# DLRM interaction and tower on one core: TensorE raises its semaphores once per several results instead of once per result

## The reference, cut to what matters

```python
# B = 2048 samples, D = 128, F = 26 tables; ids (2048, 26)
e = stack([tbl_f[ids[:, f]] for f in range(26)], axis=1)          # (B, 26, 128)
combined = concatenate([dense[:, None, :], e], axis=1)            # (B, 27, 128)
interactions = einsum('bfd,bgd->bfg', combined, combined)         # all dots of a sample's 27 vectors
z = concatenate([dense, interactions[:, IU0, IU1]], axis=1)       # the 351 pairs above the diagonal
h = concatenate([z, dense], axis=1)                               # (B, 607)
h = maximum(h @ W_top1 + b_top1, 0)                               # (B, 512)
h = maximum(h @ W_top2 + b_top2, 0)                               # (B, 256)
y = h @ W_top3                                                    # (B, 1)
```

## Time and profile before

| | |
|---|---|
| median of 3 runs | 691.15 us (689.26 to 691.96) |
| span of the profiled execution, first to last instruction | 677.5 us |
| PE busy | 423.8 us, 63% |
| POOL (gathers) busy | 275.0 us, 41% |
| DVE busy | 239.6 us, 35% |
| ACT busy | 170.0 us, 25% |
| mean granted TensorE clock | 0.758 |

### The profile page before, as it was taken

One profiled execution on the slowest core, in us unless ns is written; L12 is line 12 of the kernel. 1 busy time (PEld: TensorE's weight loads), 2 busy tenths in 40 slices (PEclk: granted clock), 3 DMA queues, 4 the chain that ended last, 5 costly groups with the idle time before them and its releaser, 6 DMA issues.

```text
span 677.5 us, 8517 instructions
## 1 busy us (share of the span) xinstructions
PE 423.8 (63%) x2992; PEld 403.1 (59%) x2992; DVE 239.6 (35%) x700; ACT 170.0 (25%) x366; POOL 275.0 (41%) x297
## 2 busy tenths in 40 slices
PE   2525354856947279471795726957269571784997
PEld 2415253855946179471794726956269471783997
DVE  5725210762504335043260432603434052530334
ACT  2204120431314024030231401313023040230551
POOL 6771737054172701727017271172712727036000
PEclk9967676786986659766597665976679575896899
DMA  8930211431114311243012430124301152001440
GB/s 222 275 93 14 71 31 50 83 108 43 51 52 83 90 29 44 55 86 87 15 48 53 81 92 12 54 51 81 94 28 48 52 99 74 19 23 50 85 64 23
DMA packets 61247, 46.01 MB, mean 68 GB/s; under 512 B 45677, under 2 KB 51301, under 8 KB 61228
## 3 DMA queue, kind: packets, MB, share of 16 engines
q1 hardware_dynamic: 52012, 26.87, 17.8%
q0 software_dynamic: 9216, 18.89, 10.8%
HBM read 37.20 MB, written 8.53 MB: 67 GB/s over the span
## 4 chain that ended last, share of the span: by engine, by line
PE 49%; another core or an unknown queue 34%; issue 11%; ACT 2%; DMA 2%; DVE 2%; SPq 1%; ACTq 0%; DVEq 0%
PE looked_up L406 20%; PE dot_bank L445 9%; PE mlp_bank L465 7%; PE mlp_bank L498 3%; PE turned L427 3%; PE turned L445 3%; PE looked_up L427 2%; DMA whole_tables<-in_tbl 2%; PE mlp_bank L508 1%; ACT dots L591 1%; PE dot_bank L427 1%; DVE whole_hidden L773 1%; ACT high_tables L635 1%; DVE combined L739 0%
## 5 line engine op out<-in xcount | busy, mean ns | idle before, releaser
L372 POOL DMA_INDIRECT rows<-in_tbl,tile_ids x288 | 273.7, 950 | 347.0 <-DVE tile_ids L736 262.4
L406 PE MATMUL looked_up<-one_hot,high_tables 125*128 125x256 f32 x512 | 144.0, 314 | 46.0 <-issue 23.4
L445 PE MATMUL dot_bank<-combined 128*108 128x108 f32 x768 | 99.4, 287 | 77.9 <-issue 41.8
L406 PE MATMUL looked_up<-one_hot,low_tables 125*128 125x256 f32 x512 | 141.6, 310 | 8.1 <-issue 8.1
L723 DVE TENSOR_SCALAR one_hot<-spread_ids,chunk_row 128x256 fp32r<-128x256 int32 x448 | 126.5, 359 | 52.6 <-remote 42.2
L406 PEld LDWEIGHTS looked_up<-one_hot,high_tables 125*128 125x128 f32 x512 | 113.0, 221 | 49.0 <-issue 49.0
L445 PEld LDWEIGHTS dot_bank<-combined 128*108 128x108 f32 x768 | 90.3, 197 | 84.1 <-issue 46.0
L406 PEld LDWEIGHTS looked_up<-one_hot,low_tables 125*128 125x128 f32 x512 | 112.7, 220 | 8.9 <-issue 8.9
L591 ACT COPY dots<-dot_bank 108x432 f32<-108x432 f32 x96 | 49.3, 519 | 242.3 <-remote 151.7
L773 DVE TENSOR_SCALAR whole_hidden<-mlp_bank,bias 128x256 f32<-128x256 f32 x28 | 13.5, 481 | 161.5 <-remote 99.1
L445 PE MATMUL turned<-combined 128*108 128x108 f32 x256 | 33.8, 281 | 47.2 <-issue 47.2
(11 more groups left out here) (73 smaller groups left out, 451.9 us busy)
## 6 DMA issues: line engine op xcount, KB each, us to landing
spread_ids<-in_ids_by_feature SPq DMA_DIRECT2D x28, 256.0 KB
scratch<-dots SPq DMA_DIRECT2D x28, 208.0 KB
rows<-in_tbl,tile_ids POOLq DMA_INDIRECT x288
whole_tables<-in_tbl SPq DMA_DIRECT2D x8, 448.0 KB
whole_hidden<-scratch SPq DMA_DIRECT2D x24, 117.0 KB
scratch<-dots SPq DMA_DIRECT2D x28, 52.0 KB
rows<-in_r_dense_features SPq DMA_DIRECT2D x16, 64.0 KB
first_ids<-in_ids_by_feature SPq DMA_DIRECT2D x1, 896.0 KB, 8.5
```

The source lines that it names most:

```text
L372: nc.gpsimd.indirect_dma_start(rows[:, u, slot, :], None, tables[f][:, :], bass.IndirectOffsetOnAxis(ap=tile_ids[:, u, slot - 1:slot], axi ...
L406: last = nc.tensor.matmul(looked_up[n % 2][:, 0:COLS], parts[part][0:ROWS_K, n, c, :], one_hot[0:ROWS_K, n % HOT, c, :], start=(c == 0 and ...
L445: last = nc.tensor.matmul(dot_bank[b % DOT_BANKS][0:SQUARE, q * SQUARE:(q + 1) * SQUARE], quad, quad, start=True, stop=True)
```

## The change

TensorE's signals are merged; a merged signal adds as many counts as it stands for, so that the readers' counts stay as they were. Transposes signal after group 1 (two counts) and after group 4 (three). Dots signal after fills 2, 5 and 7 (three, three and two counts). `half_used` is gone; `product_done` is raised after every second look-up by two, two look-ups now share one PSUM bank (256 columns each), and a look-up of an even number from 4 on waits for the copies of all look-ups up to number `n - 3`. Layer 1 signals after outputs 1 and 3 by two, layer 2 once by two, and the last block's layer 1 once by four. Readers are unchanged but for the one-hots, which wait once, for `product_done` of look-up `n-3`.

```diff
+LOOKS_PER_BANK = 2
+TURNED_SIGNALS = {1: 2, N_GROUPS - 1: N_GROUPS - 2}
+DOTS_SIGNALS = {2: 3, 5: 3, 7: 2}
...
-        half_used = sem("half_used")
...
+        def look_view(n):
+            at = n % LOOKS_PER_BANK * COLS
+            return looked_up[n // LOOKS_PER_BANK % 2][:, at:at + COLS]
...
-                    if n >= 2:
-                        pe.wait_ge(product_copied, m * N_PRODUCT + n - 1)
+                    if n >= 2 * LOOKS_PER_BANK and n % LOOKS_PER_BANK == 0:
+                        pe.wait_ge(product_copied, m * N_PRODUCT + n - LOOKS_PER_BANK)
...
-                        if c == CHUNKS // 2 - 1:
-                            last.then_inc(half_used, 1)
-                    last.then_inc(product_done, 1)
+                    if n % LOOKS_PER_BANK == LOOKS_PER_BANK - 1:
+                        last.then_inc(product_done, LOOKS_PER_BANK)
...
-                    last.then_inc(turned_done, 1)
+                    if g in TURNED_SIGNALS:
+                        last.then_inc(turned_done, TURNED_SIGNALS[g])
...
-                    last.then_inc(dots_done, 1)
+                    if b in DOTS_SIGNALS:
+                        last.then_inc(dots_done, DOTS_SIGNALS[b])
...                                                            (layer1)
-                    last.then_inc(layer_done, 1)
+                    if o % 2 == 1:
+                        last.then_inc(layer_done, 2)
...                                                            (last_layer1)
-                    if tiles[-1] == K_TILES - 1:
-                        last.then_inc(layer_done, 1)
+                if tiles[-1] == K_TILES - 1:
+                    last.then_inc(layer_done, LAYER1)
...                                                            (layer2)
-                    last.then_inc(layer_done, 1)
+                last.then_inc(layer_done, LAYER2)
...                                                            (make_one_hots)
                     if n >= HOT and c == 0:
-                        dve.wait_ge(half_used, m * N_PRODUCT + n - HOT + 1)
-                    if n >= HOT and c == CHUNKS // 2:
                         dve.wait_ge(product_done, m * N_PRODUCT + n - HOT + 1)
```

More of the change, by code:

```diff
@@ L400, in look_up_products @@
                         pe.wait_ge(table_split, n + 1)
-                    if n >= 2:
-                        pe.wait_ge(product_copied, m * N_PRODUCT + n - 1)
+                    if n >= 2 * LOOKS_PER_BANK and n % LOOKS_PER_BANK == 0:
+                        pe.wait_ge(product_copied, m * N_PRODUCT + n - LOOKS_PER_BANK)
                     for c in range(CHUNKS):
                         for part in (HIGH, LOW):
-                            last = nc.tensor.matmul(looked_up[n % 2][:, 0:COLS], parts[part][0:ROWS_K, n, c, :],
+                            last = nc.tensor.matmul(look_view(n), parts[part][0:ROWS_K, n, c, :],
                                                     one_hot[0:ROWS_K, n % HOT, c, :],
@@ L563, in copy_products @@
                     act.wait_ge(product_done, m * N_PRODUCT + n + 1)
-                    nc.scalar.copy(combined[:, 0, :, PRODUCT_SLOT + n], looked_up[n % 2][:, 0:P])
-                    nc.scalar.copy(ahead[:, n, :], looked_up[n % 2][:, P:COLS]).then_inc(product_copied, 1)
+                    nc.scalar.copy(combined[:, 0, :, PRODUCT_SLOT + n], look_view(n)[:, 0:P])
+                    nc.scalar.copy(ahead[:, n, :], look_view(n)[:, P:COLS]).then_inc(product_copied, 1)
             def move_ahead(m, products):
```

## The result

The changed kernel takes 729.68 us (median of 4 runs, 723.71 to 733.46) where the kernel before took 690.2 us beside it (median of 4): ratio 1.0581, 95% interval 1.0503 to 1.0660, 39.5 us slower. The forecast was 733 us and 42.1 us slower. The profiled execution is the one of 733.46 us.

The account below looks back on a forecast made before the run. TensorE's matmuls were taken to wait in line beside two gathers a block, so merging only costs: 16.1 + 5.0 + 7.0 + 4 + 4 + 6 = 42.1 us, giving 733 us; the range was 683 to 748.

Parts of the forecast that it names:

- Matmuls wait, not signals: TensorE beside a gather: matmuls queue whether or not they carry signals, so fewer signals shorten nothing; chance 0.72, 733 us.
- the step of 1.3 us: TensorE's line of some 32 matmuls beside a gather was read as moving one by one, about 1.3 us each.
- The layer pair: Layer 1: outputs 2 and 3 both run after the gather, delaying 5 gathers by 2.7 us; 16.1 us with the last block.
- the end: Last layers: relus waiting for the last output about 1.7 us, block 6's layers 1.4, layer 2's two relus 0.6.
- That delays the transposes of tile 0 and the ids of the next gather: After layer 1's output 3: transposes end at 302.23, ids follow at 302.85, so the next gather starts 2.7 us later.
- Look-ups: One-hots wait for look-up pairs and VectorE becomes the bound: 16.4 us a block, 1.0 more, 7.0 us for seven blocks.
- Dots: Three signals a tile: fills wait for whole groups; 4 us over 5 gathers, 4 in blocks 0 and 1, 2.4 in the last.
- transposes: Group 2's copy waits for group 4, so ids come 0.55 us later before 9 gathers not otherwise counted: 5.0 us.
- The base: Profiled span of 677.5 us plus 42.1 gives 719.6; adding 13.65 us between span and median of runs gives 733.
- Signals as the slow thing: Rival, chance 0.16: beside a gather the line serves signals alone, 6.6 us each, so merging is faster, near 640 us.
- Partly so: Rival, chance 0.08: a signal takes as much of the line as two or three matmuls; 695 us, between 675 and 715.
- All hidden: Rival, chance 0.04: all held signals are hidden, so no change, 691 us.

Follow-up runs that it names:

- no half-way signal: Kernel before with `half_used` alone removed, look-ups still signalling one by one and one-hot n waiting for look-up n-3: 687.53 us, ratio 1.0017.
- fourth bank: Kernel before with a fourth PSUM bank for the dots (`turned[0]`), signals as before: 682.56 us, ratio 0.9906.
- moved gather: Kernel before with the gather of `u` = 0 started only once SyncE had issued the block's loads of the pairs: 657.15 us, ratio 0.9586.
- the last two together: Kernel before with both a fourth PSUM bank for the dots and the later start of the `u` = 0 gather: 657.45 us, ratio 0.9581.

## Why the prediction was right, point by point, and where it was not

**Matmuls wait, not signals: right.** It was read from eight single issues in the earlier trace rows; four times the signals at no cost and twice the matmuls with half the fills reported show it, and 32 matmuls were counted in the line a second time. What the prediction took from one stretch and is not general is the step of 1.3 us.

**The layer pair: its mechanism right, its sum wrong.** A to B grew by 2.3 to 3.0 us before each of the five gathers B (2.7 forecast) with the 24 matmuls behind the gather. Alone, though, the whole edit cost 3.5 us (7.3 by the medians) and not the 19.8 of its parts (16.1 in the blocks, 3.7 of the end), since the five stretches from B to A became 8.0 us shorter. In that trace the end came out near the forecast, 5.5 us longer where 2.6 and 3.7 were forecast. The failed step is "That delays the transposes of tile 0 and the ids of the next gather", taken as if all that follows moves with it: the dots began sooner against B, and more of them were reported within it. In the full change the stretch from B to the look-ups did not become shorter (30.2 to 30.8 us; before 28.9 to 30.9, with layer pairs alone 23.0 to 29.4). There fills 0 to 2 are copied from +5.7 on as well, but fills 3 to 5 share one report, and that comes at the release, +25.6; with the layer pairs alone the fill after these three was reported at +13.6. So the merged dots seem to take back what the layer pairs alone had given.

**Look-ups: the term that was mis-sized, 7 forecast, 18.5 measured alone.** From the end of the first pair on VectorE is the bound, as I wrote. But the sum of a block, 16.4, lacked three things that the trace after shows: the last look-up takes 2.19 us instead of 1.93, each of the three hand-overs costs 0.17, and the five one-hots take 10.77 instead of 10.6: 17.3 with them, as measured (358.14 to 375.46). At the half clock the first pair is longer by 1.4 us, uncovered. And blocks 0 and 1, which I counted as one ordinary block each, carry about 8 us. In the changed kernel the look-ups of the five steady blocks take 89.1 us together against 84.2, 4.9 more, where 5.0 were forecast. That agreement is luck: each is longer than I summed, but three of the five before took 17.6 to 17.9 us and not 15.5, since they began at the half clock, and after the change four of the five run at the full clock throughout.

**Dots 8.8 against 10.4, transposes 6.1 against 5.0:** within their bounds. Of the whole by stretches: the five periods cost 25.6 us, and the forecast's terms for them (13.5 of layer pairs, 5 of look-ups, 4 of dots, 2.75 of transposes) are 25.3. The stretches from A to B are 13.7 of it against 13.5. The last stretch cost 10.6 against 8.6. The start cost 17.9 against 8.2, of which 1 to 4 us lie in the profiled execution of before: its gather A of block 1 began at 183.2, and in six other kernels (more signals, layer pairs, no half-way signal, fourth bank, moved gather, the last two together) at 184.0 to 187.0.

**The base: a wrong step that happened to do little.** I took the 13.65 us between the profiled span and the median as what lies around a span. It is 1.9 us (733.46 less 731.6, and as much in every run here that shows both). The kernel before spreads from 679.1 to 694.2 us, and its profiled execution was one of the shortest. So the profiled span is 12 us over the forecast one of 719.6, while the difference of the medians, 42.1 forecast against 39.5, hardly noticed. The total was right partly by luck: by the runs of single parts the layer pairs were too dear by 12 to 16 us and the look-ups too cheap by 11.

**The rivals.** Signals as the slow thing is refuted. Partly so (a signal worth two or three matmuls) does not fit the run with four times the signals either, where 24 more a tile left the time as it was, and it would have wanted the report of output 1 inside the gather; its relu ran with output 0's, behind the release at 316.8. All hidden is refuted by the interval. What the trace was to show came: groups of 3, 3, 2, the last pair at +25.6, 24 matmuls behind the hole. Only the look-ups came out as 17.3 and not 16.4.

**The rule against it.** The Trainium skill, "TensorE: Matmul & The Clock Gate", section "The cost: per-tile semaphore tail", has increments serialize at 26.3 ns each; 384 more would be 10 us, an estimate from the page, if they were on the path. The kernel with them took 0.1% to 0.9% less than the one before, so nothing of it is on the path here. The prediction says that rows 6 bear the size out where no gather runs; they show only ScalarE's 0.24 us between copies and price no increment.

**Open.** Why the line of matmuls moves at different speeds within a gather, what in a gather holds it (its transfers or their issuing), why one third fill of 14 comes late (+10.9) though the dots start first, and where the 8 us of blocks 0 and 1 arise.

## What to carry to other kernels

A signal that nobody waits for cost nothing here, and a signal that comes later costs whatever its reader could have done in between: merge signals only where the reader would wait for the last of the group anyway, and count the buffers, since three buffers and pairs make two engines go in step. Where a transfer slows one engine's reports, look at which work stands beside it: work that needs an answer after every few instructions is better placed elsewhere, and one wait that moves the transfer gave 4.1% where no change to the signals gave more than 0.5%. Try such parts together as well as alone: here one part seems to have taken back what another had gained. Take a kernel's base from the median, and a profiled span with what lies around it, measured and not inferred.

## What the runs showed of the hardware that was not expected

Beside 18 indirect DMAs (25.4 to 25.6 us from the first to the release), TensorE's reports fall behind in all kernels. The cost of a block's two gathers, 40 to 45 us (41.2 without them, 81 to 86 with them), is as much as GpSimd's own time in them, 44.4 us. The line is counted in matmuls, holds 31 or 32 of them in both places where it was counted, and slows within a gather: 0.24, 0.45, then 1.15 us a matmul in the kernel with twice the matmuls. One microsecond goes with much at its start: where the dots began no later than a gather's first DMA their third fill was copied by +6.2 in 13 of 14 blocks, where they began 0.8 us or more after it only at +12.1 to +22.1. And 384 additional increments of a semaphore by TensorE are not measurable in 687 us.
